# Pairwise attention scoring on one Trainium2 core: two score visits of four steps per fill, transposes before round 8

## The reference

```python
V = emb_v[x]                              # 32 x 2048 x 64
VV = V[iu] * V[ju]                        # 496 pairs
hid = relu(einsum('pbk,kh->pbh', VV, at_w) + at_b)
score = einsum('pbh,ho->pbo', hid, at_h)
pooled = sum(VV * score, axis=0)
prob = sigmoid(pooled @ p + w0 + sum(w1[x], axis=0))
```

## Time and profile before

| | us |
|---|---|
| median of 3 runs | 843.54 (842.78 to 846.02) |
| span of the profiled execution, first to last instruction | 835.8 |
| PE busy | 784.1 (94%) |
| DVE busy | 722.5 (86%) |
| ACT busy | 640.7 (77%) |
| POOL busy | 555.4 (66%) |

### The profile page before, as it was taken

The page is one execution under the profiler, slowest core; times in us unless marked ns, Lnnn a source line. Parts: engine busy times, 40 slices in busy tenths (PEclk is TensorE's granted clock), DMA queues, the critical chain, the costliest instruction groups (busy, mean ns, idle before and its releaser), DMA issues.

```text
span 835.8 us, 26345 instructions
## 1 busy us (share of the span) xinstructions
PE 784.1 (94%) x10550; PEld 277.6 (33%) x10550; DVE 722.5 (86%) x1221; ACT 640.7 (77%) x674; POOL 555.4 (66%) x537
## 2 busy tenths in 40 slices
PE   0488996999999999999999999999999999999998
PEld 0123332333333333333333333333333333333332
DVE  4278897699999999999999999999999999999894
ACT  0267775788798887878878788898888888888785
POOL 5577777666677676666766766677667666766720
PEclk9989998999999999999999999999999999999999
DMA  7533268445423466544332347644434457633200
GB/s 257 99 25 24 26 22 25 23 22 22 23 22 23 20 22 23 21 22 24 21 22 22 23 21 22 23 24 21 22 21 23 21 22 23 24 22 22 11 1 1
DMA packets 19398, 24.27 MB, mean 29 GB/s; under 512 B 9960, under 2 KB 10029, under 8 KB 19373
## 3 DMA queue, kind: packets, MB, share of 16 engines
q0 software_dynamic: 16896, 17.07, 43.4%
q1 hardware_dynamic: 1535, 6.64, 2.1%
q10 hardware_dynamic: 942, 0.22, 0.1%
HBM read 20.59 MB, written 3.31 MB: 29 GB/s over the span
## 4 chain that ended last, share of the span: by engine, by line
PE 86%; DMA 5%; POOL 5%; issue 2%; ACT 1%; DVE 0%; ACTq 0%; POOLq 0%
PE Z L591 52%; PE SG L607 26%; POOL rows L303 5%; PE SG L621 4%; PE Z L553 4%; DMA rows<-table,joint_idx 3%; DMA rows<-in_L_rec_emb_v_dram,idx 2%; ACT pV L471 0%; ACT H L526 0%; DMA idx_raw<-in_r_x_dram 0%; PE Z L685 0%; ACT V L460 0%; PE Z L664 0%; ACT y_sb L537 0%; ACTq L247 0%
## 5 line engine op out<-in xcount | busy, mean ns | idle before, releaser
L303 POOL DMA_INDIRECT rows<-table,joint_idx x496 | 518.8, 1046 | 224.0 <-issue 139.7
L445 DVE TENSOR_TENSOR X<-V 128x992 f32<-128x992 f32 (+15 forms) x1024 | 635.6, 692 | 28.8 <-ACT V L500 14.8
L526 ACT ACTIVATE H<-Z,bias 128x1024 f32<-128x1024 f32 x512 | 529.7, 1121 | 113.2 <-PE Z L591 109.8
L591 PE MATMUL Z<-X,w_sb 64*64 64x512 f32 x4096 | 477.2, 600 | 7.4 <-DVE X L445 3.4
L591 PEld LDWEIGHTS Z<-X,w_sb 64*64 64x64 f32 x4096 | 147.0, 132 | 288.7 <-issue 283.2
L607 PE MATMUL SG<-H,score_w 128*32 128x512 f32 x2048 | 239.4, 597 | 0.0
L607 PEld LDWEIGHTS SG<-H,score_w 128*32 128x32 f32 x2048 | 56.8, 109 | 172.8 <-issue 96.0
L471 ACT ACTIVATE pV<-V,pmask 128x1024 f32<-128x1024 f32 x64 | 81.5, 1276 | 0.1
L413 DVE TENSOR_TENSOR prod<-SG,gram 128x512 f32<-128x512 f32 x32 | 22.1, 691 | 63.3 <-PE SG L607 63.3
L460 ACT COPY V<-Z 128x1024 f32<-128x1024 f32 x31 | 31.4, 1013 | 42.4 <-PE Z L553 42.4
L621 PEld LDWEIGHTS SG<-V,pV 128*32 128x32 f32 x4096 | 42.7, 109 | 23.9 <-issue 19.3
(11 more groups left out here) (46 smaller groups left out, 35.1 us busy)
## 6 DMA issues: line engine op xcount, KB each, us to landing
rows<-table,joint_idx POOLq DMA_INDIRECT x496, 3.7
table<-joined SPq DMA_DIRECT2D x4, 792.0 KB
H<-in_L_rec_emb_v_dram SPq DMA_DIRECT2D x4, 768.0 KB, 8.3
rows<-in_L_rec_emb_v_dram,idx POOLq DMA_INDIRECT x16, 5.3
w_all<-in_L_rec_w_dram,idx POOLq DMA_INDIRECT x16
idx_raw<-in_r_x_dram SPq DMA_DIRECT2D x2, 64.0 KB, 2.1
idx_raw<-in_r_x_dram ACTq DMA_DIRECT2D x2, 64.0 KB, 2.3
table<-tail SPq DMA_DIRECT2D x1, 54.7 KB
```

Source lines behind the costliest of these rows:

```text
L303: pool.indirect_dma_start(out=rows[t % 2][:, g * FILL_M + m, half, c0:c1], out_offset=None, in_=source, in_offset=bass.IndirectOffsetOnAxi ...
L445: last_one = nc.vector.tensor_tensor(xo, vj, vi.unsqueeze(3).to_broadcast(shape), ALU.mult)
L526: nc.scalar.activation(H[:, s % H_SLOTS, :, COLS * g:COLS * g + COLS], Z[:, z_slot(t, r), :, :], ACT.Relu, bias=bias[:, 0:1]).then_inc(hid ...
L591: done = nc.tensor.matmul(Z[64 * par:64 * par + 64, z_slot(t, r), half, :], w_sb[k, :], X[k, s % X_SLOTS, par, COLS * g:COLS * g + COLS], ...
```

## The change

Five constants change. `SCORED_AFTER` goes from three visits (2 steps of the fill before after round 5; 3 steps after round 11; 3 steps after round 15) to two (4 steps of the fill before after round 7; 4 steps after round 15). The turn moves from before round 6 to before round 8, directly behind the first visit as it was; in fills 1 and 2 from before round 12 to before round 11. With `TURN_BEFORE`, `TURN_SLOT` goes from 0 to 2, and the rounds with a wait for the relu of two rounds earlier go with the turn, on PE and (the copy of V) on ACT. The last fill leaves steps 4 to 7 for the end, where it left 6 and 7. All instructions stay the same in kind and number.

```diff
-TURN_BEFORE, LATE_TURN = 6, 12
+TURN_BEFORE, LATE_TURN = 8, 11
 LATE_FILLS = (1, 2)
 LOOP_BEFORE = 2
-SCORED_AFTER = {5: (-1, (6, 7)), 11: (0, (0, 1, 2)), 15: (0, (3, 4, 5))}
-LAST_STEPS = (6, 7)
+SCORED_AFTER = {7: (-1, (4, 5, 6, 7)), 15: (0, (0, 1, 2, 3))}
+LAST_STEPS = (4, 5, 6, 7)
```

## The result

The changed kernel takes 889.43 us (median of 4, 887.87 to 892.38) where the kernel before had 843.16 (4 runs: the three of before and one more, of 839.35): ratio **1.0566**, 95% interval 1.0533 to 1.0598. It is slower, as forecast, and the forecast of 889.5 (876 to 904) is hit nearly to the point. The misses cancel.

What follows compares the result with a forecast made beforehand. PE was taken to bound the kernel, held to ACT's 1.00 us per relu in stretches over four rounds. Loop +45.1, start -3.5 and last fill +4.4 gave +46.0 on 843.5: 889.5 us, range 876 to 904.

Steps and rivals of the forecast that it cites:

- Rounds 6 and 7 at the relu distance: First half of a fill: two added rounds each cost ACT's 1.00 us between relus, so 5.48 becomes 7.48.
- Turn to last visit: Second half: X from DVE and relu 12 from ACT both hold round 15, so the visit starts 9.9 us after the turn.
- T + 7.4: Round 15's start without ACT's hold: 7.4 us after the turn's start T, instead of 8.9.
- Where the waits show: PE's timeline in the loop: idle of about 1.5 us ahead of round 15 and nowhere else.
- The loop: Fills 4 to 31: each of 27 fills grows by 1.67 us, from 24.09 to 25.76, giving +45.1.
- The last fill: Fill without a turn, ending in eight score steps: 27.85 us instead of 23.38, so +4.4.
- The start: Before fill 4: a shorter wait for rows in fill 3 makes fill 4 start 3.5 us earlier, bounds -5 to 0.
- What lies around the span: Start and end of an execution outside the profiled span: 7.7 us, unchanged, within the base of 843.5.
- fewer drains: Rival: PE keeps its own 0.86 us a round in long stretches; fill 23.44, time 824, chance 0.04.
- a shorter hold: Rival: ACT and DVE are each 1.0 us earlier at round 15; fill 24.76, time 861.5, chance 0.06.
- waits that add up: Rival: more rounds wait, with up to 0.5 us lost at round 15; fill 26.4 to 26.8, 906 to 917, chance 0.07.
- The clock: Rival: the 1.5 us hold at round 15 brings half clock in each fill; +92 us, time 981, chance 0.03.

Runs made afterwards that it cites:

- e1b: Changed kernel with DVE's weigh moved from before X of round 10 to round 14, sum from 12 to 15; 882.04 us, ratio 1.0524.
- e2b: Changed kernel with ACT's pV and w1 copies put before the relus of rounds 14 and 15 in every fill; 892.49 us, ratio 1.0625.
- e3b: Changed kernel with both DVE's weigh and sum moved later and ACT's pV and w1 copies moved; 844.56 us, ratio 1.0095.
- e1: Changed kernel with DVE's weigh and sum moved to before X of rounds 14 and 15, on the slow chip; 1126.86 us, ratio 1.0146.
- e3: Changed kernel with both DVE's weigh and sum and ACT's pV and w1 copies moved, on the slow chip; 1096.63 us, ratio 0.9885.

## Why the prediction was right, point by point

- **Rounds 6 and 7 at the relu distance**: 7.48 forecast, 7.49 measured. Right.
- **First visit**: 3.57 forecast and 3.57 measured; **last visit** 3.46 and 3.46; **grams** 1.35 and 1.34. Right.
- **Turn to last visit**: 9.9 forecast, 9.92 measured, and for the reason given. That two engines hold round 15 "to the same tenth" is shown by e1b and e2b (each hold removed alone: 9.84 and 9.90 from the turn to the last visit, 25.73 and about 25.77 a fill) with e3b (both removed: 8.51 and 24.38). The T + 7.4 for round 15 without the hold is 0.1 low by the prediction's own steps, which give relu 12 an end at T + 7.4 and round 15 a start 0.1 later; its expectation of 8.5 for the visit has it right.
- **Where the waits show**: wrong. I said a gap ahead of round 15 "and nowhere else in the loop". DVE makes X at 1.23 a round from round 12 on, so PE is already late at round 12 (0.56 in the bracket) and follows DVE's pace; only with DVE's hold gone (e1b) does the gap stand ahead of round 15. I had computed when the X of round 15 is done but not those of 12 to 14. The sum did not depend on it. ACT's wait ahead of relu 0 was forecast at some 4 and is 2.99; DVE's ahead of `weigh` at 3.4 and is 3.57.
- **The loop**: forecast 27 x 1.67 = +45.1. Measured from the start of fill 4 to that of fill 31, 854.06 - 158.08 = 695.98 against 652.46: +43.5. The fill itself is right: the changed kernel's alternate between 25.72 and 25.78, 25.75 on average against the forecast 25.76, and those before are 24.10 on average without two long ones; 27 x 1.65 is +44.6. The rest is that the kernel before lost 1.2 us in its fill 4, whose first six rounds took 6.66 instead of 5.48, with the late instructions shown above among them, and the changed one lost no such time there. The prediction had the sign of it in hand, 24.17 a fill on average against the 24.09 that it subtracted, and did not use it.
- **The last fill**: 27.85 forecast; 854.06 to 881.91 is 27.85.
- **The start**: failed. -3.5 forecast, 158.08 - 154.25 = +3.8 measured. Fill 3 was forecast to start at 123.3 and started at 130.63. Of these 7.3 us, 5.38 are the idle in the grams and 2.0 come before it, from fill 1, whose turn waited 2.50 us for rows where that of the kernel before waited for none. Then the rounds at half clock cost 1.7 more, and the 1.6 that the turn of fill 3 was to wait for rows fell away. The step that failed is that the start follows from waits for rows and for X alone; "an idle stretch of 1.6 should not bring it" looked at the wait for rows, which indeed vanished, and not at PE's instructions, so the sign named for the start (a clock of 1.00 in fill 3) came out wrong as well.
- **What lies around the span**: wrong. The 7.7 us that the text ahead of the prediction gives to start and end of an execution compare two different executions. An execution takes 1.85 more than its span (889.45 against 887.6); the profiled execution of the kernel before was thus about 837.7, near the medians of 837.3 to 838.2 that this kernel had in the three later sets of runs, on two other chips. Between the two profiled spans the change is 887.6 - 835.8 = +51.8, made of +3.8, +43.5, +4.5 and nothing behind. I forecast +46.0. The 889.5 came out because the start was forecast 7.3 too short, the loop 1.6 too long and the base about 6 too high.
- **The rivals**: fewer drains (refuted by e3b, even without the holds), a shorter hold (refuted by 9.92), waits that add up (round 15 loses nothing to its two waits). The clock fell nowhere in the loop (1.00 from 160 to 880); it did at the start, in the idle of 5.38.

## What to carry to other kernels

Where PE works between two engines (DVE makes its input, ACT empties its output) that are each slower than it in a stretch but need less than PE over the whole fill, other work of PE between the stretches is what lets them catch up. Lengthening the stretches to save changes of kind costs the difference in pace per round, here 1.00 less 0.86 for each round past the fourth, and 1.4 more (25.78 less 24.38) where side jobs stand in both queues. Write the start of each item down for every feeding engine, not only for the last item, and look for two chains that end together: removing one shows nothing, and a single-edit experiment would have called each of them harmless. And check what lies around the span against a known pair of execution and span before adding it to a base.

## What the runs showed that was not expected

PE's instructions came late in seven of the profiles between 121 and 136 us, by 1.1 to 5.4 us, while gathers kept the DMA engines busy (0.84 in the changed kernel), and with the half clock behind it this cost the changed kernel about 7 us. On one chip the same kernels ran a third slower (1114.55 for the kernel before), with PE idle far more in every profile while DVE's busy time in e1 was 723.5 us, as elsewhere. On that chip the order of the variants changed: e3 was 1.2% faster than the kernel before (interval 0.2% to 2.1%), where e3b is 1.0% slower. What is said here of a schedule balanced to a tenth of a microsecond is shown for the chips on which the kernel before takes 835 to 846 us.
